# A cross-attention and feed-forward block on one Trainium2 core: the ramp's work in another order, part of w2 loaded from ScalarE's queue, three multiplications on GpSimd

## The chip, the cores and the metric

The kernel runs on one core of one Trainium2 chip. The metric is the device time of one execution in microseconds (us), the median of several runs. Engines: TensorE (PE, matrix products), VectorE (DVE), ScalarE (ACT), GpSimd (POOL) and SyncE (SP), which here only starts transfers. The kernel is written with explicit semaphores: each engine has one list of instructions, worked in the order of the code, and an instruction waits until the semaphores named ahead of it have reached their values.

## The reference

```python
# x (4, 2048, 512), ctx (4, 154, 512); _layernorm is (x - mean) / sqrt(var + eps)
def xattn(x, context, Wq, Wkv, Wout, bout):        # 16 heads of 64
    q = x @ Wq; k, v = split(context @ Wkv)
    mask = j_idx % n_q == i_idx                    # n_q = 2048, n_kv = 154
    sim = where(mask, q k^T * scale, -max)
    return softmax(sim) @ v  @ Wout + bout
def ffn(x, w1, b1, w2, b2, gamma, beta):
    h = layernorm(x, gamma, beta)
    h = qlinear(h, w1, b1)      # y = xq . wq / (sx * sw) + b
    h = gelu(h, approximate=False)
    return qlinear(h, w2, b2)
# act_quant:    scale = 127 / max|x| of the row, xq = round(x * scale)
# weight_quant: scale = 1 / mean|w|, wq = clip(round(w * scale), -1, 1)
x = x + xattn(_layernorm(x), ctx, Wq, Wkv, Wout, bout)
x = x + ffn(_layernorm(x), w1, b1, w2, b2, gamma, beta)
```

Row i below 154 of a batch may see context row i alone, so its attention is that row's value; every other row sees only masked entries, all alike, and gets the mean value of the context. The attention is therefore a row `ctx[i] @ Wv @ Wout + bout` for 154 rows of a batch and one mean row for the others.

## The kernel before

The 8192 rows of x are cut into 64 tiles `t` of 128 rows, rolled by two tiles, so that the first tiles are such that need only batch 0's mean row. The **ramp**, some 100 us, prepares the weights and runs the first tiles between; then a loop over steps `s` runs tile `s`'s first layer and tile `s - 3`'s second layer.

Preparation:
- *Mean row.* TensorE sums batch 0's context (`context_mean`), VectorE scales it (`copy_ctx_mean`). For each of the eight 128-row chunks m of Wv's transpose, `mean_product(m)` (L710) multiplies the chunk with the mean context into one of three buffers `product[m % 3]`, ScalarE's `mean_sum(m)` (L536) sums it along the row, and `mean_weighted(m)` (L717, L721) adds the chunk of Wout times that sum. TensorE's `mean_row` (L990) adds over partitions and VectorE's `mean_row` (L727) writes the result with bout. GpSimd's additions to x wait for it.
- *Wv Wout.* TensorE's `products` (L983) makes `wvo` in 32 products, read from PSUM by ScalarE's `copy_wvo` (L558). `out_rows(i)` (L1008) multiplies a batch's context `ctxm` with wvo, and `attn_rows(i)` (L843) stores it; `tail_product` (L1016) and `tail_rows_out` (L746) serve context rows 128 to 153, with column sums from `ctx_sum` and `ctx_means`.
- *Weights.* w1 comes in eight pieces. ScalarE's `abs_w1(i)` (L543) sums |w| of six, VectorE's (L751) of two. `weight_sum(0)` (L758), TensorE's `weight_total(0)` (L995) and `weight_scale(0)` (L762) give the scale. Then `round_w1` (VectorE, L769) and `round_weights(0, n)` (ScalarE, L553) round, and `clip(0, n)` (VectorE, L779) bounds to -1 and 1. w2 goes the same way in eight pieces: `abs_w2` and `round_weights(1, n)` on ScalarE, `clip(1, n)` on VectorE.

A tile: `add_attention` (GpSimd, L387), `statistics` (VectorE, L784, L786), `inverse_std` (GpSimd, L391, L394), `centre` (VectorE, L792: (x - mean) * gamma), `times_std` (ScalarE, L563), `add_beta` (GpSimd, L402), `x_scale` (VectorE, L797 to L804), `round_x` (ScalarE, L569), `widen_x` and `scale_rows` (GpSimd), a transposing transfer `transpose_x` (SyncE), `bias` and `first_layer` (TensorE, L1030, L1040; 16 products), `gelu` (ScalarE, L578, two halves), `half_scale` and `hidden_scale` (VectorE, L809, L815: row maxima), `round_h` (ScalarE, L587), `transpose_h` (SyncE), `widen_h` in two halves (VectorE L829, ScalarE L596), `second_layer` (TensorE, L1055; 16 products) and `result` (VectorE, L838).

The order in the ramp is written out by hand for each engine: SyncE's from L267, GpSimd's from L439, ScalarE's from L600, VectorE's from L845, TensorE's from L1060. What waits for what around the change:
- `weight_sum(0)` for six abs_w1 on ScalarE and two on VectorE; `weight_total(0)` stands between TensorE's products 30 and 31 of 32.
- `centre(t)` (from t = 6) for `round_x(t - 6)`; ScalarE's `times_std(t)` for `centre(t)` and GpSimd's `inverse_std`.
- `second_layer(0)` for both halves of `widen_h(0)`, for the tail rows, and half by half for the clips of w2; `second_layer(t)` for `widen_h(t)`.
- raw w2 pieces 0 and 3 use the places of x tiles 12 to 15, piece 1 that of the int8 hidden rows, 2 and 4 those of the transposed hidden tiles, 5 to 7 that of Wout, so these wait for `mean_done`, `wvo_done` and the like.

```python
            def out_rows(i):
                b = (i + 1) % B
                pe.wait_ge(wvo_copied, KD)
```

Here `out_rows` needs all four copies of wvo before its first product.

Of the kernel before, what the change touches and what calls it, by code (L numbers as in the profile page):

```python
# [8 lines left out]
ALU = mybir.AluOpType  # L9
# [3 lines left out]
P = 128  # L13
# [5 lines left out]
KD, KI = D // P, INNER // P  # L19
# [14 lines left out]
def block_program(nc, x, ctxm_d, ctxt_d, wvT, wout_d, bout, w1T, b1, w2T, b2, gamma, beta, ctx_b0, out, tail_rows, b1_pieces):  # L34
    es = ExitStack()
    with es:
# [6 lines left out]
        def sem(name):  # L43
            return es.enter_context(nc.semaphore(name))
# [50 lines left out]
        ctx_mean = hx[:, 2, 0, :]  # L95
# [29 lines left out]
        vprod_dve = sem("vprod_dve")  # L125
# [67 lines left out]
        def _(sp):  # L193
# [114 lines left out]
            load_x(9)  # L308
            sp.dma_start(b2_b[:, 0, :], b2.partition_broadcast(P)).then_inc(b2_loaded, 16)
            load_x(10)  # L310
            transpose_x(1)
# [3 lines left out]
            transpose_x(2)  # L315
            transpose_x(3)
            transpose_x(4)
            transpose_h(0)
            transpose_x(5)
            load_x(14)  # L320
            transpose_h(1)
            load_x(15)
# [32 lines left out]
        def _(pool):  # L355
# [94 lines left out]
            inverse_std(2, 2)  # L450
            add_attention(4, 1)
            add_beta(1, 1)
            add_attention(5, 1)
            widen_x(0, 1)
            pool.wait_ge(wscale_done[0], 1)
            scale_rows(0, 1)
            add_beta(2, 1)
            add_beta(3, 1)
            inverse_std(4, 2)
            scale_rows(1, 1)  # L460
            add_attention(6, 1)
            widen_x(1, 1)
            add_beta(4, 1)
            add_beta(5, 1)
            scale_rows(2, 2)
            widen_x(2, 2)
            add_attention(7, 1)
            add_attention(8, 1)
            scale_rows(4, 2)
            add_attention(9, 1)  # L470
            pool.wait_ge(b2_loaded, 16)
            add_b2(0)
            inverse_std(6, 2)
# [49 lines left out]
        def _(act):  # L523
# [92 lines left out]
            copy_wvo(2)  # L616
            times_std(1)
            abs_w1(6)
            abs_w1(7)
            round_x(0)  # L620
            times_std(2)
            times_std(3)
            abs_w2(0)
            copy_wvo(3)
            round_weights(0, 1)
            round_weights(0, 3)
            abs_w2(1)
            times_std(4)
            times_std(5)
            round_x(1)  # L630
            abs_w2(2)
            abs_w2(4)
            abs_w2(3)
# [3 lines left out]
            gelu(0, 0)  # L637
            round_x(2)
            gelu(0, 1)
            round_x(3)  # L640
            round_weights(1, 0)
            round_weights(1, 1)
            round_x(4)
            round_x(5)
            gelu(1, 0)
            gelu(1, 1)
            round_h(0)
            round_weights(1, 2)
            round_weights(1, 3)
            round_weights(1, 4)  # L650
            gelu(2, 0)
            times_std(6)
            gelu(2, 1)
            round_h(1)
            round_weights(1, 5)
            round_weights(1, 6)
            widen_h(0)
            round_weights(1, 7)
            times_std(7)
            gelu(3, 0)  # L660
            gelu(3, 1)
            round_h(2)
# [36 lines left out]
        def _(dve):  # L699
# [148 lines left out]
            mean_product(2)  # L848
# [4 lines left out]
            mean_product(4)  # L853
            mean_product(5)
            mean_weighted(3)
            mean_product(6)
# [10 lines left out]
            statistics(1)  # L867
            statistics(2)
            statistics(3)
            abs_w1(4)  # L870
            centre(1)
            centre(2)
            x_scale(0, 1)
            centre(3)
            statistics(4)
            weight_sum(0)
            centre(4)
            weight_scale(0)
            statistics(5)
            x_scale(1, 1)  # L880
            ctx_sum(0)
            ctx_sum(1)
            ctx_sum(2)
            centre(5)
            x_scale(2, 2)
            attn_rows(0)
            ctx_sum(3)
            round_w1(0)
            round_w1(2)
            clip(0, 0)  # L890
            clip(0, 1)
            clip(0, 2)
            clip(0, 3)
            attn_rows(1)
            attn_rows(2)
            weight_sum(1)
            ctx_means()
            weight_scale(1)
            x_scale(4, 2)
            half_scale(0)  # L900
            statistics(6)
            statistics(7)
            hidden_scale(0)
            half_scale(1)
            statistics(8)
            statistics(9)
            hidden_scale(1)
            centre(6)
            centre(7)
            half_scale(2)  # L910
            attn_rows(3)
            tail_rows_out()
            hidden_scale(2)
            clip(1, 0)
            clip(1, 1)
            clip(1, 2)
            clip(1, 3)
            widen_h(0)
            clip(1, 4)
            clip(1, 5)  # L920
            clip(1, 6)
            clip(1, 7)
# [40 lines left out]
        def _(pe):  # L963
# [117 lines left out]
            tail_product()  # L1081
# [55 lines left out]
```

## Time and profile before

| | |
|---|---|
| median of 3 runs | 539.83 us (539.54 to 540.08) |
| the profiled execution's own time | 540.51 us |
| its span, first to last instruction | 538.7 us |
| mean granted TensorE clock | 0.990 |
| TensorE busy | 527.3 us, 98% |
| VectorE, ScalarE, GpSimd busy | 453.6 (84%), 435.9 (81%), 407.3 (76%) |
| moved by the queues | 78.72 MB, mean 146 GB/s |

Busy time of an engine is the time in which an instruction of it ran. Rows of a timeline give start, length, engine, line of the code, operation, what it writes and reads and how many merged instructions the row holds; "idle before" in square brackets is the engine's idle time ahead of the row and what released it. An fp32 product is two passes on TensorE, so its rows count two. The granted clock is a share of 2.4 GHz. A transfer's time to landing runs from its issue to the last byte.

### The profile page before, as it was taken

Reading aid. Unit: us, or ns where it says so; the run is one execution under the profiler, and the core shown is the slowest. Engines: PE = TensorE matmul, PEld = TensorE weight load, DVE = VectorE, ACT = ScalarE, POOL = GpSimd, SP = SyncE. Lnnn points to the kernel's source line nnn. Section 1 sums busy time; section 2 is a strip of 40 time slices with the busy share of each in tenths; the row PEclk is TensorE's granted clock in tenths of the full one; section 3 lists DMA queues with packets and bytes.
Section 4 is the critical chain, followed back from the end, with each engine's and each line's share of the span. In section 5 each row is a group of like instructions: output and inputs, shape, how many; then the busy total and the mean of one; then the engine's idle time right before and its main releaser. Section 6 shows DMA issues by size and latency. Waiting matters only on the chain.

```text
span 538.7 us, 8129 instructions
## 1 busy us (share of the span) xinstructions
PE 527.3 (98%) x2434; PEld 227.4 (42%) x2434; DVE 453.6 (84%) x758; ACT 435.9 (81%) x444; POOL 407.3 (76%) x533
## 2 busy tenths in 40 slices
PE   9979989999999999999999999999999999999997
PEld 5433434444444444444444444444444444444443
DVE  3877999999989899988888887988888889887653
ACT  3558899888887888888888888888888889887762
POOL 2288687999998888888888988888888888873300
PEclk9987999999999999999999999999999999999999
DMA  8999233886565656555665556665455574535433
GB/s 310 402 387 294 69 69 102 170 208 162 135 122 141 131 148 119 129 125 130 131 143 142 123 129 117 141 132 132 124 123 130 129 142 103 92 86 100 95 78 98
DMA packets 137015, 78.72 MB, mean 146 GB/s; under 512 B 114246, under 2 KB 114310, under 8 KB 136972
## 3 DMA queue, kind: packets, MB, share of 16 engines
q1 hardware_dynamic: 135636, 75.80, 57.3%
q10 hardware_dynamic: 1335, 2.41, 1.3%
q8 instruction: 19, 0.31, 0.2%
q14 instruction: 25, 0.20, 0.1%
HBM read 33.88 MB, written 17.05 MB: 95 GB/s over the span
## 4 chain that ended last, share of the span: by engine, by line
PE 95%; DVE 3%; POOL 1%; ACT 1%; issue 1%; POOLq 0%; DVEq 0%; ACTq 0%
PE py L1055 41%; PE p L1040 28%; PE pab L1040 14%; PE p L983 3%; PE p L1030 3%; PE pab L1008 2%; PE pab L1030 1%; POOL xr L387 1%; PE pab L968 1%; DVE hx L792 1%; PE py L1016 1%; PE py L1008 1%; DVE w2q L779 1%; ACT hid L578 0%; PE py L974 0%
## 5 line engine op out<-in xcount | busy, mean ns | idle before, releaser
L1055 PE MATMUL py<-w2q,hqT 128*128 128x512 bf16 x1024 | 231.0, 379 | 1.7 <-DVE hqT L829 1.7
L587 ACT ACTIVATE hq<-hid,hscale 128x2048 int8<-128x2048 f32 x64 | 128.1, 2002 | 46.2 <-DVE hscale L821 46.2
L1040 PE MATMUL p<-w1q,xqT 128*128 128x512 bf16 x688 | 159.4, 380 | 0.0
L1055 PEld LDWEIGHTS py<-w2q,hqT 128*128 128x128 bf16 x1024 | 100.1, 98 | 123.0 <-DVE hqT L829 2.7
L578 ACT ACTIVATE hid<-p,xdeq 128x1024 f32<-128x1024 f32 x86 | 95.0, 1106 | 15.9 <-PE p L1040 11.2
L1040 PEld LDWEIGHTS p<-w1q,xqT 128*128 128x128 bf16 x688 | 63.8, 98 | 81.2 <-issue 10.1
L387 POOL TENSOR_TENSOR xr<-xr,attn 128x512 f32<-128x512 f32 x64 | 83.3, 1320 | 18.7 <-DVE attn L727 17.2
L402 POOL TENSOR_TENSOR hx<-hx,beta_b 128x512 f32<-128x512 f32 x64 | 91.7, 1454 | 4.4 <-ACT hx L563 4.3
L815 DVE TENSOR_REDUCE hmax<-hid 128x1 f32<-128x1025 f32 x64 | 78.1, 1220 | 18.0 <-ACT hid L578 17.4
L406 POOL TENSOR_TENSOR xr<-xr,b_b 128x512 f32<-128x512 f32 x64 | 92.6, 1465 | 0.0
L809 DVE TENSOR_REDUCE hid<-hid 128x1 f32<-128x1024 f32 x64 | 77.4, 1209 | 8.8 <-ACT hid L578 8.8
L829 DVE CAST hqT<-hT 128x1024 bf16<-128x1024 int8 x64 | 61.5, 962 | 23.4 <-PE py L1055 12.9
L1040 PE MATMUL pab<-w1q,xqT 128*128 128x512 bf16 x336 | 79.6, 380 | 0.0
L596 ACT ACTIVATE hqT<-hT 128x1024 bf16<-128x1024 int8 x64 | 67.0, 1046 | 3.1 <-DMA hT<-hq 3.1
L433 POOL CAST xq<-xq 128x1024 bf16<-128x1024 int16 (+1 forms) x33 | 34.3, 1039 | 44.8 <-ACT xq L569 44.8
L792 DVE SCALAR_TENSOR_TENSOR hx<-xr,mv,gamma_b 128x512 f32<-128x512 f32 x64 | 54.1, 849 | 0.1
L578 ACT ACTIVATE hid<-pab,xdeq 128x1024 f32<-128x1024 f32 x42 | 46.5, 1106 | 7.2 <-PE pab L1040 3.9
L838 DVE SCALAR_TENSOR_TENSOR xr<-py,hdeq,xr 128x512 f32<-128x512 f32 x64 | 47.4, 740 | 3.3 <-PE py L1055 3.3
L1040 PEld LDWEIGHTS pab<-w1q,xqT 128*128 128x128 bf16 x336 | 31.1, 98 | 39.5 <-issue 4.8
L563 ACT ACTIVATE hx<-hx,rstd 128x512 f32<-128x512 f32 x64 | 42.7, 715 | 5.9 <-POOL rstd L394 5.3
L784 DVE BATCH_NORM_STATS2 stat<-xr 128x6 f32<-128x512 f32 x64 | 43.0, 672 | 3.4 <-POOL xr L387 3.3
L569 ACT ACTIVATE xq<-hx,xscale 128x512 int16<-128x512 f32 x64 | 42.6, 714 | 0.1
(88 smaller groups left out, 408.9 us busy)
## 6 DMA issues: line engine op xcount, KB each, us to landing
xr<-x SPq DMA_DIRECT2D x64, 256.0 KB, 2.9
out<-xr SPq DMA_DIRECT2D x64, 256.0 KB, 2.4
raw<-w1T SPq DMA_DIRECT2D x8, 512.0 KB, 12.2
hid<-wvT SPq DMA_DIRECT2D x8, 256.0 KB, 7.8
wout<-wout_d ACTq DMA_DIRECT2D x8, 256.0 KB, 8.7
wout<-w2T SPq DMA_DIRECT2D x3, 512.0 KB, 5.5
xr<-w2T SPq DMA_DIRECT2D x2, 512.0 KB, 11.1
attn<-ctxm_d SPq DMA_DIRECT2D x4, 256.0 KB, 8.1
```

What stands on the lines that cost most here:

```text
L387: pool.tensor_tensor(xtile(t, n), xtile(t, n), a, ALU.add).then_inc(x1_ready, n)
L402: pool.tensor_tensor(htile(t, n), htile(t, n), bb, ALU.add).then_inc(xnormed, n)
L406: pool.tensor_tensor(xtile(t), xtile(t), b2_b[:, :, :], ALU.add).then_inc(xb_ready, 1)
L578: nc.scalar.activation(hid[:, t % 2, h * HALF:(h + 1) * HALF], hidden_pair(t, h), ACT.Gelu, scale=col(xdeq, t)).then_inc(gelu_done, 1)
L587: nc.scalar.activation(hq8[:, t % 2, :], hid[:, t % 2, 0:HID], ACT.Copy, scale=col(hscale, t))\
L596: nc.scalar.activation(hqT[:, t % 2, NJ // 2:, :, :], hT8[:, t % 2, HALF:].rearrange("p (j t e) -> p j e t", e=2, t=P), ACT.Copy).then_inc ...
L792: nc.vector.scalar_tensor_tensor(htile(t)[:, 0, :], xtile(t)[:, 0, :], mv[:, t % 8, 0:1], gamma_b[:, :], ALU.subtract, ALU.mult).then_inc( ...
L809: nc.vector.tensor_reduce(hid[:, t % 2, HID:HID + 1], hid[:, t % 2, 0:HALF], AX.X, ALU.max, apply_absolute_value=True).then_inc(hmax_half, 1)
L815: nc.vector.tensor_reduce(col(hmax, t), hid[:, t % 2, HALF:HID + 1], AX.X, ALU.max, apply_absolute_value=True).then_inc(hmax_done, 1)
L829: nc.vector.tensor_copy(hqT[:, t % 2, 0:NJ // 2, :, :], hT8[:, t % 2, 0:HALF].rearrange("p (j t e) -> p j e t", e=2, t=P))\
L1040: mm = nc.tensor.matmul(hidden_bank(t, n), xT[:, k, :], w1q[:, k, n * D:(n + 1) * D], start=False, stop=(k == KD - 1))
L1055: mm = nc.tensor.matmul(py[:, t % 2, :], hqT[:, t % 2, c // 2, c % 2, :], w2q[:, c, :], start=(c == 0), stop=(c == 2 * NJ - 1))
```

## The change

It does five things.

1. GpSimd makes `mean_product` for chunks 2, 4 and 6, counted by a semaphore of its own; VectorE keeps the other five. ScalarE's `mean_sum` waits for the one or the other.
2. w2's pieces 0 to 4 are started by ScalarE, between its steps; 5 to 7 stay with SyncE.
3. `out_rows` waits for each copy of wvo ahead of the product that reads it.
4. SyncE asks for w1's last pieces before x tile 3, and for the context and b1's rows before x tiles 4 to 6; `transpose_x(1)` to `(3)` and x tiles 14 and 15 move.
5. The lists of all five engines in the ramp are put in another order; on TensorE `out_rows(2)` and `(3)`, `weight_total(1)` and `tail_product` change places with tiles' layers. The loops from step 6 on stay.

```diff
@@ SyncE
-                if j == 3:
-                    sp.wait_ge(mean_done, 1)
...
-            load_x(3)
             load_w1(6)
             load_w1(7)
+            load_x(3)
+            load_ctx()
+            load_b1_rows()
             load_x(4)
-            load_w2(0)
-            load_b1_rows()
             load_x(5)
-            load_w2(1)
-            load_ctx()
-            load_w2(2)
             load_x(6)
-            load_w2(3)
-            load_w2(4)
             transpose_x(0)
             load_w2(5)
             load_w2(6)
+            transpose_x(1)
             load_w2(7)
@@ GpSimd
+            def mean_product(m):
+                pool.wait_ge(chunk_loaded[m], 32)
+                pool.wait_ge(ctx_mean_copied, 1)
+                if m >= 3:
+                    pool.wait_ge(vmean_done, m - 1)
+                pool.tensor_tensor(product[m % 3], wv[:, m // 4, m % 4, :], ctx_mean, ALU.mult).then_inc(vprod_pool, 1)
...
             split_b1()
+            mean_product(2)
+            mean_product(4)
+            mean_product(6)
             pool.wait_ge(mean_copied, 1)
             add_attention(0, 1)
             add_attention(1, 1)
-            add_attention(2, 1)
-            add_attention(3, 1)
             pool.wait_ge(const_set, 3)
             inverse_std(0, 1)
+            add_attention(2, 1)
             inverse_std(1, 1)
@@ ScalarE
+            def load_w2(j):
+                if j == 3:
+                    act.wait_ge(mean_done, 1)
+                act.dma_start(w2raw[j], w2T[j * 2 * P:(j + 1) * 2 * P, :].rearrange("(p e) n -> p e n", e=2))\
+                    .then_inc(w2_loaded[j], 16)
...
-                act.wait_ge(vprod_dve, m + 1)
+                if m in (2, 4, 6):
+                    act.wait_ge(vprod_pool, m // 2)
+                else:
+                    act.wait_ge(vprod_dve, (1, 2, 0, 3, 0, 4, 0, 5)[m])
@@ TensorE
                 b = (i + 1) % B
-                pe.wait_ge(wvo_copied, KD)
...
                 for k in range(KD):
+                    pe.wait_ge(wvo_copied, k + 1)
...
             bias(0)
-            out_rows(2)
             first_layer(0, 0)
             first_layer(0, 1)
-            weight_total(1)
+            out_rows(2)
             bias(1)
             first_layer(1, 0)
+            weight_total(1)
             first_layer(1, 1)
-            out_rows(3)
+            tail_product()
             bias(2)
             first_layer(2, 0)
             first_layer(2, 1)
-            tail_product()
+            out_rows(3)
```

VectorE from the clips of w2 (L779, `w2q<-w2q`) to its fourth `half_scale` (`hid<-hid`), in the order before:

```order
L779 TENSOR_SCALAR w2q<-w2q 128x1024 x4
L829 CAST hqT<-hT 128x1024
L779 TENSOR_SCALAR w2q<-w2q 128x1024 x4
L784 BN_STATS stat<-xr 128x6
L786 BN_AGGR mv<-stat 128x2
L792 SCALAR_TENSOR_TENSOR hx<-xr,mv,gamma_b 128x512
L784 BN_STATS stat<-xr 128x6
L786 BN_AGGR mv<-stat 128x2
L809 TENSOR_REDUCE hid<-hid 128x1
```

and of the change, what stands between the last clip and the same `half_scale`:

```order
L811 SCALAR_TENSOR_TENSOR hx<-xr,mv,gamma_b 128x512
L803 BN_STATS stat<-xr 128x6
L805 BN_AGGR mv<-stat 128x2
L803 BN_STATS stat<-xr 128x6
L805 BN_AGGR mv<-stat 128x2
L811 SCALAR_TENSOR_TENSOR hx<-xr,mv,gamma_b 128x512
L803 BN_STATS stat<-xr 128x6
L805 BN_AGGR mv<-stat 128x2
L811 SCALAR_TENSOR_TENSOR hx<-xr,mv,gamma_b 128x512
L803 BN_STATS stat<-xr 128x6
L805 BN_AGGR mv<-stat 128x2
L828 TENSOR_REDUCE hid<-hid 128x1
```

Before, only statistics(10), centre(8) and statistics(11) stand between the last clip and that row; now it is centre(6) to (8) and statistics(8) to (11). The clips themselves moved ahead, in pairs, among other steps.

ScalarE from its first |w1| sum on (L543 or L557, `w1q,wpart<-raw`), before:

```order
L543 ACTIVATE w1q,wpart<-raw 128x1024
L563 ACTIVATE hx<-hx,rstd 128x512
L543 ACTIVATE w1q,wpart<-raw 128x1024
L558 ACTIVATE wvo<-p 128x512
L563 ACTIVATE hx<-hx,rstd 128x512
L543 ACTIVATE w1q,wpart<-raw 128x1024 x2
L569 ACTIVATE xq<-hx,xscale 128x512
```

and now:

```order
L557 ACTIVATE w1q,wpart<-raw 128x1024
L536 DMA xr<-w2T 128x1024
L536 DMA hq<-w2T 128x1024
L577 ACTIVATE hx<-hx,rstd 128x512
L557 ACTIVATE w1q,wpart<-raw 128x1024
L536 DMA hqT<-w2T 128x1024
L536 DMA xr<-w2T 128x1024
L572 ACTIVATE wvo<-p 128x512
L557 ACTIVATE w1q,wpart<-raw 128x1024
L536 DMA hqT<-w2T 128x1024
L583 ACTIVATE xq<-hx,xscale 128x512 x2
```

Five transfers of w2 stand between the sums of w1's last pieces, and both `round_x` of tiles 0 and 1 follow at once.

## Rows read from the trace of the kernel before

**Rows 1.** Table of stretches: start:end, length, busy (and count) by engine, PEclk, DMA, GB/s.
```profile
22.25:84.51 62.26, 55.21 (x176) 23.03 (x174) 54.05 (x96) 50.85 (x68) 49.60 (x62) 0.92 0.65 215
84.51:103.00 18.49, 18.49 (x92) 7.78 (x88) 18.01 (x30) 16.48 (x17) 16.10 (x20) 1.00 0.57 128
...
120.00:200.00 80.00, 80.00 (x395) 34.27 (x393) 74.60 (x125) 69.01 (x68) 70.39 (x90) 1.00 0.61 139
```

**Rows 2.** Timeline of TensorE, 21 to 107 us.
```profile
21.09 1.05 PE L990 MATMUL py<-xr,hT 128*128 128x512 f32 x2
21.98 12.18 PE L983 MATMUL p<-wout,hid 128*128 128x512 f32 x28
37.66 0.56 PE L995 MATMUL py<-wsum,hT 128*128 128x1 f32 x2 [3.50 <-DVE wsum L758]
38.08 3.76 PE L983 MATMUL p<-wout,hid 128*128 128x512 f32 x4
42.53 9.30 PE L1008 MATMUL pab<-wvo,attn 128*128 128x512 f32 x16 [0.69 <-ACT wvo L558]
...
64.32 3.60 PE L1008 MATMUL py<-wvo,attn 128*128 128x512 f32 x8
...
80.81 3.63 PE L1055 MATMUL py<-w2q,hqT 128*128 128x512 bf16 x16 [1.68 <-DVE hqT L829]
...
103.03 3.63 PE L1055 MATMUL py<-w2q,hqT 128*128 128x512 bf16 x16
```

**Rows 3.** Table of stretches of 2 us, columns as in rows 1.
```profile
36.00:38.00 2.00, 0.34 (x2) 0.37 (x2) 1.97 (x5) 2.00 (x5) 2.00 (x3) 0.67 1.07 401
38.00:40.00 2.00, 2.00 (x5) 0.97 (x5) 1.11 (x4) 1.39 (x3) 2.00 (x3) 0.50 1.03 399
```

**Rows 4.** Timeline of VectorE, 14 to 104 us.
```profile
14.27 1.29 DVE L710 TENSOR_TENSOR hx<-hid,hx 128x512 f32<-128x512 f32 x2
...
22.25 0.69 DVE L727 TENSOR_TENSOR attn<-py,bout_b 128x512 f32<-128x512 f32 x1 [1.29 <-PE py L990]
...
70.00 3.20 DVE L792 SCALAR_TENSOR_TENSOR hx<-xr,mv,gamma_b 128x512 f32<-128x512 f32 x2
...
84.51 1.19 DVE L809 TENSOR_REDUCE hid<-hid 128x1 f32<-128x1024 f32 x1
...
89.40 0.77 DVE L792 SCALAR_TENSOR_TENSOR hx<-xr,mv,gamma_b 128x512 f32<-128x512 f32 x1
...
101.83 1.75 DVE L829 CAST hqT<-hT 128x1024 bf16<-128x1024 int8 x2
```

**Rows 5.** Waits of VectorE, 22 to 103 us: total, times, longest.
```profile
DVE stat L784 <- POOL xr L387: 3.3, 4, 1.8
DVE attn L843 <- PE pab L1008: 2.6, 1, 2.6
```

**Rows 6.** Timeline of GpSimd, 22 to 36 us.
```profile
23.02 4.20 POOL L387 TENSOR_TENSOR xr<-xr,attn 128x512 f32<-128x512 f32 x3 [17.19 <-DVE attn L727]
28.70 1.26 POOL L387 TENSOR_TENSOR xr<-xr,attn 128x512 f32<-128x512 f32 x1 [1.48 <-DMA xr<-x]
```

**Rows 7.** Timeline of ScalarE, 30 to 81 us.
```profile
30.93 0.72 ACT L563 ACTIVATE hx<-hx,rstd 128x512 f32<-128x512 f32 x1 [5.34 <-POOL rstd L394]
...
75.70 2.19 ACT L553 ACTIVATE w2q<-wout,wscale 128x1024 int16<-128x1024 f32 x2
...
79.66 1.13 ACT L553 ACTIVATE w2q<-wout,wscale 128x1024 int16<-128x1024 f32 x1
```

**Rows 8.** SyncE's last issue of w1 and last two of ctxm: ns, first and last start.
```profile
L206 SPq DMA_DIRECT2D raw<-w1T x1: 1123/1123/1123, 19.3 to 19.3; - x1
...
DMA to landing us min/median/max: 11.9/11.9/11.9
...
L220 SPq DMA_DIRECT2D attn<-ctxm_d x2: 432/434/435, 29.9 to 30.4; - x2
...
DMA to landing us min/median/max: 7.4/8.0/8.6
```

More of the change, by code:

```diff
@@ L124, in block_program @@
         ctx_mean_done, ctx_mean_copied = sem("ctx_mean_done"), sem("ctx_mean_copied")
-        vprod_dve = sem("vprod_dve")
+        vprod_dve, vprod_pool = sem("vprod_dve"), sem("vprod_pool")
         vmean_done, mean_part_done = sem("vmean_done"), sem("mean_part_done")
@@ L308, in _ @@
             load_x(9)
+            transpose_x(2)
+            transpose_x(3)
             sp.dma_start(b2_b[:, 0, :], b2.partition_broadcast(P)).then_inc(b2_loaded, 16)
             load_x(10)
-            transpose_x(1)
             load_x(11)
@@ L314, in _ @@
             load_x(13)
-            transpose_x(2)
-            transpose_x(3)
+            transpose_h(0)
+            load_x(14)
+            load_x(15)
+            transpose_h(1)
             transpose_x(4)
-            transpose_h(0)
             transpose_x(5)
-            load_x(14)
-            transpose_h(1)
-            load_x(15)
             transpose_h(2)
@@ L449, in _ @@
             add_beta(0, 1)
-            inverse_std(2, 2)
-            add_attention(4, 1)
             add_beta(1, 1)
-            add_attention(5, 1)
+            add_attention(3, 1)
             widen_x(0, 1)
@@ L456, in _ @@
             scale_rows(0, 1)
+            inverse_std(2, 2)
+            widen_x(1, 1)
+            scale_rows(1, 1)
             add_beta(2, 1)
             add_beta(3, 1)
+            add_attention(4, 1)
+            scale_rows(2, 2)
+            add_attention(5, 1)
+            add_attention(6, 1)
+            widen_x(2, 2)
             inverse_std(4, 2)
-            scale_rows(1, 1)
-            add_attention(6, 1)
-            widen_x(1, 1)
+            add_attention(7, 1)
             add_beta(4, 1)
             add_beta(5, 1)
-            scale_rows(2, 2)
-            widen_x(2, 2)
-            add_attention(7, 1)
             add_attention(8, 1)
@@ L470, in _ @@
             add_attention(9, 1)
+            inverse_std(6, 2)
             pool.wait_ge(b2_loaded, 16)
             add_b2(0)
-            inverse_std(6, 2)
             add_attention(10, 1)
@@ L615, in _ @@
             abs_w1(5)
-            copy_wvo(2)
+            load_w2(0)
+            load_w2(1)
             times_std(1)
             abs_w1(6)
+            load_w2(2)
+            load_w2(3)
+            copy_wvo(2)
             abs_w1(7)
+            load_w2(4)
             round_x(0)
+            round_x(1)
+            round_weights(0, 1)
+            copy_wvo(3)
+            round_weights(0, 3)
             times_std(2)
@@ L623, in _ @@
             abs_w2(0)
-            copy_wvo(3)
-            round_weights(0, 1)
-            round_weights(0, 3)
             abs_w2(1)
-            times_std(4)
-            times_std(5)
-            round_x(1)
             abs_w2(2)
+            abs_w2(3)
+            gelu(0, 0)
             abs_w2(4)
-            abs_w2(3)
+            gelu(0, 1)
+            round_x(2)
+            round_x(3)
             abs_w2(5)
@@ L636, in _ @@
             abs_w2(7)
[L637 to L644, printed above, removed]
             gelu(1, 0)
             gelu(1, 1)
+            round_weights(1, 0)
+            times_std(4)
+            times_std(5)
+            round_weights(1, 1)
             round_h(0)
@@ L649, in _ @@
             round_weights(1, 3)
+            gelu(2, 0)
             round_weights(1, 4)
-            gelu(2, 0)
-            times_std(6)
             gelu(2, 1)
@@ L655, in _ @@
             round_weights(1, 5)
+            round_x(4)
+            round_x(5)
+            widen_h(0)
             round_weights(1, 6)
-            widen_h(0)
             round_weights(1, 7)
-            times_std(7)
             gelu(3, 0)
             gelu(3, 1)
+            times_std(6)
+            times_std(7)
             round_h(2)
@@ L847, in _ @@
             mean_product(1)
-            mean_product(2)
             mean_product(3)
@@ L852, in _ @@
             mean_weighted(2)
-            mean_product(4)
             mean_product(5)
             mean_weighted(3)
-            mean_product(6)
             mean_product(7)
@@ L867, in _ @@
             statistics(1)
+            centre(1)
+            abs_w1(4)
             statistics(2)
-            statistics(3)
-            abs_w1(4)
-            centre(1)
             centre(2)
             x_scale(0, 1)
-            centre(3)
[L875 to L880, printed above, removed]
+            weight_sum(0)
+            x_scale(1, 1)
+            weight_scale(0)
+            round_w1(0)
+            clip(0, 0)
+            statistics(3)
+            centre(3)
+            clip(0, 1)
+            round_w1(2)
+            clip(0, 2)
+            clip(0, 3)
+            attn_rows(0)
             ctx_sum(0)
@@ L883, in _ @@
             ctx_sum(2)
-            centre(5)
[L885 to L900, printed above, removed]
+            x_scale(2, 2)
+            ctx_sum(3)
+            attn_rows(1)
+            half_scale(0)
+            ctx_means()
+            hidden_scale(0)
+            statistics(4)
+            weight_sum(1)
+            centre(4)
+            weight_scale(1)
+            attn_rows(2)
+            statistics(5)
+            centre(5)
+            half_scale(1)
+            hidden_scale(1)
+            clip(1, 0)
+            clip(1, 1)
             statistics(6)
             statistics(7)
-            hidden_scale(0)
-            half_scale(1)
+            x_scale(4, 2)
+            tail_rows_out()
+            clip(1, 2)
+            clip(1, 3)
+            half_scale(2)
+            hidden_scale(2)
+            clip(1, 4)
+            clip(1, 5)
+            widen_h(0)
+            attn_rows(3)
+            clip(1, 6)
+            clip(1, 7)
+            centre(6)
             statistics(8)
             statistics(9)
-            hidden_scale(1)
-            centre(6)
             centre(7)
[L910 to L922, printed above, removed]
             statistics(10)
```

## The prediction

> **What bounds the kernel now.** I read the table of stretches first, then TensorE's rows of the ramp with the granted clock, then what VectorE and ScalarE waited for. TensorE is busy 80.00 of 80.00 us in the steady part, and 18.49 of 18.49 already from 84.51 on [rows 1]. The change touches nothing that TensorE does there. So only the ramp can give time, and only if `second_layer(3)`, which starts at 103.03 [rows 2], starts earlier and no gap opens behind it.
>
> TensorE's losses in the ramp stand as idle time in its rows: 3.50 us ahead of `weight_total(0)` at 37.66, 0.69 ahead of `out_rows(0)`, 1.68 ahead of `second_layer(0)` at 80.81 [rows 2]. The long one has a second price. The granted clock is 0.67 in 36 to 38 and 0.50 in 38 to 40 [rows 3]: it fell to 1.2 GHz inside that gap. The four passes behind it took 3.76 where 28 took 12.18 (1.74 for four), and sixteen passes of `out_rows` took 9.30 where eight at 2.4 GHz take 3.60 [rows 2]: 2.0 and 2.1 more. With these three gaps TensorE alone could win 10 us.
>
> It is not alone. `second_layer(3)` needs VectorE's `widen_h(3)`, the first of two casts that fill 101.83 to 103.58 [rows 4]; TensorE comes to it at 103.0 straight from tile 6. Both arrive together, and VectorE is busy 18.01 of the 18.49 us before [rows 1]. The end is held twice, and the second holder is VectorE's list.
>
> **The decisive step: VectorE's list.** From `mean_row` (22.25) to `half_scale(3)` (84.51) [rows 4] both orders hold the same work (statistics 0 to 11, centre 0 to 8, all clips, attn_rows 0 to 3), arranged differently; from `half_scale(3)` to `widen_h(3)` nothing is moved. The three multiplications that leave VectorE lie ahead of 22.25, where it waits 1.29 for TensorE anyway [rows 4]: they give nothing here. In the stretch VectorE is busy 54.05 of 62.26 [rows 1] and idle 8.2: 3.3 and 2.6 are its two large waits [rows 5], 2.3 small waits and the short steps between dependent instructions. The change can give 8.2 minus the idle time that it leaves.
>
> **New times, step by step.**
> GpSimd makes `inverse_std(0)` behind two additions, not four. Three additions take 4.20 from 23.02; the fourth ends at 29.96 [rows 6], and ScalarE's `times_std(0)` follows at 30.93 [rows 7], 0.97 later. Now it is 23.02 + 2.80 + 0.97 = 26.8; ScalarE's 5.34 us of waiting go. Late next is the rest of ScalarE's own list up to the last abs_w1: three of these at the 1.05 of a 1024-column step (two take 2.19 with 0.1 of overlap [rows 7]), two small steps and copy_wvo, some 0.6 each, and four DMA issues. An issue is 0.43 on SyncE [rows 8]. That is 26.8 + 3.15 + 1.8 + 1.7 = 33.5. w1's last piece landed at 31.2 (19.3 + 11.9 [rows 8]) and is now asked for before x tile 3. `weight_sum(0)` so moves from 37.4 to 33.6, TensorE is free at 34.16, and the 3.50 us gap closes, with it the fall of the clock.
>
> The products end at 36.2. The context has to be in; it was at 39.0 (30.4 + 8.6 [rows 8]). It now stands right behind x tile 3, 1.2 MB after 31.2, which is 3.1 us at the 400 GB/s that rows 3 show: 34.3 alone. But w2's pieces 0 and 1 (1 MB, 2.6 us) enter beside it on ScalarE's queue: 36.9. The DMA share is 1.07 and the rate 401 GB/s in 36 to 38 [rows 3]: the pipe is full, so a second queue only lets w2 in ahead of what SyncE's queue holds. I take 0.8 us of TensorE waiting at `out_rows(0)`, ends 0 and 2.6; the five issues cost ScalarE 5 x 0.43 = 2.2. The Trainium skill, "DMA: Bandwidth & Descriptors", section "Issuing engines are not separate DMA queues", goes against this part in the same way: starting transfers from several engines saves issue time only. By that rule it gains nothing on the wire and moves issue time from an idle queue to a busy engine; the trace's full rate agrees.
>
> From 37.0: two `out_rows` 7.2, tile 0's layer 3.9, `out_rows(2)` 3.6, half of tile 1's layer 2.1: 53.8. `weight_total(1)` needs all eight abs_w2, and ScalarE's list (two large roundings, four small steps, eight abs, two gelu) ends there too. Then half a layer, and `gelu(1,1)` is done at 56.9. Behind it ScalarE has, without a wait, eight roundings and two gelu at 1.05, four small steps at 0.6, two `round_h` of twice that width at 1.9 and a `widen_h` of 1: 17.7. The last of w2 is rounded at 74.6; it was 80.7 (79.66 + 1.13, less overlap [rows 7]). `second_layer(0)` starts near 73.
>
> But 6 us won there are not 6 us. In the old order centre(6) and (7) and statistics(6) to (9) were done **ahead** of the w2 clips, in time in which VectorE would have waited for ScalarE. Now centre(6), statistics(8), (9), centre(7), statistics(10), centre(8), statistics(11) follow clip(1,7). Four statistics at about 0.8, and three centres at 0.77 (alone) to 1.60 (3.20 for two, beside GpSimd [rows 4]), are 5.5 to 8.0, which puts `half_scale(3)` at 80.5 to 83.0. The other account goes by waits: 0.3 before statistics(0), 1.0 around weight_sum(0), 0.9 before weight_sum(1), 3.8 where clips 5 to 7 come at ScalarE's pace, and 1.5 for what lies between dependent instructions: 7.5. Then 22.25 + 54.05 + 7.5 = 83.8. I take 83.8, since 54.05 contains the real stretching of this ramp by other engines, and the chain's single durations don't. That is 0.7 us before 84.51.
>
> **The three products on GpSimd.** No such multiplication is in the trace. The nearest row is GpSimd's addition of the same shape, 1.26 alone and 1.40 as one of three [rows 6]. VectorE's last step of that chain ends at 20.96 (22.25 less 1.29), and TensorE would take its result from 21.09 on [rows 2]: 0.1 us of cover. The gain can't be used. The cost is bounded by what a centre shows for two-input work on both engines, 0.8 more each (1.60 against 0.77), 2.4 for three, less the 1.9 that VectorE no longer does (three at 0.65, as in the 1.29 for two [rows 4]). I take 0.3; ends 0 and 0.9, a gain being excluded because TensorE's products last to 21.1. The Trainium skill, "GPSIMD Engine Reference", section "Key points", says that GpSimd shares its SBUF interfaces with VectorE and contends with instructions that have two SBUF inputs. The rows of the centres agree. By that rule alone this part would cost VectorE about what it saves.
>
> **Sum.** -0.7 for VectorE's list, +0.3 for the mean row: -0.4. The profiled execution took 540.51 (span 538.7) and would take 540.1. The median of the runs, 539.83, lies 0.68 below it and goes to 539.4. A measurement of this kernel can tell about 0.2%, 1.1 us, from no change, so the likeliest case would hardly be seen.
>
> **Rivals.**
> *The clock falls later (slower).* TensorE does `second_layer(0)` in two halves, the second behind clip(1,7), to 77, then tile 4 in 3.85: 81. `second_layer(1)` needs `widen_h(1)`, behind `half_scale(3)`: 83.8 + 1.1 + 0.6 = 85.5. A gap of 4 to 5 us opens where there was none. The gap of 3.50 brought the clock down [rows 2, 3]; behind the one of 1.68 sixteen passes took 3.63, as at 2.4 GHz [rows 2]. If it falls again for as long (products and two `out_rows` were hit, till some 46 us), some 8 us of work run at 1.2 GHz and lose 4.1. The slack: 85.5 and two tile steps of 7.4 (three take 22.22 from 80.81 to 103.03 [rows 2]) are 100.3, against 102.2 for VectorE. It decides once 1.9 are lost, that is 3.8 us of slow work. 100.3 + 4.1 = 104.4, 1.4 later than 103.03, and 0.3 for the mean row: 541.5; ends 540.3 and 542.5. For it: the length of the gap. Against: a ScalarE that lags moves TensorE into the gap and shortens it.
> *The centres run free (faster).* With `half_scale(3)` at 80.5, 4.0 us are to be had; ScalarE, busy 16.48 of 18.49 [rows 1], has 2.0 of room. So 2.0 to 2.5 go: 537.5. For it: the chain's own low end. Against: GpSimd has additions queued through the whole stretch.
> *Nothing moves (no change).* The context is 2.6 late, the products cost 0.9, the waits only change places: 539.8.
>
> **Chances.** Forecast 0.42, clock 0.25, free centres 0.20, nothing moves 0.13. Of the forecast 0.08 lie past 1.1 us faster; of the clock case 0.22 past 1.1 slower. Faster 0.28, same 0.50, slower 0.22. The range leaves out the outer ends of the two outer cases: 537.3 to 541.9; the forecast's own is 538.4 to 540.2.
>
> **What would show it.** Right: no idle before `weight_total(0)`, a clock of 1.00 in 36 to 48, `second_layer(0)` before 76, `half_scale(3)` at 83 to 84.5, a TensorE gap of 3 to 5 us before `second_layer(1)` put down to the hqT cast, `second_layer(3)` near 102.3. A clock of 0.5 somewhere in 83 to 93 shows the first rival. The forecast is wrong if `half_scale(3)` comes before 82.5, if TensorE shows gaps behind 110, or if the mean row is copied later than 22.8.

## The result: 0.94% slower, outside the range

| | before | after |
|---|---|---|
| median of the runs | 539.96 us (4 runs, 539.54 to 541.34) | 545.38 us (4 runs, 541.82 to 547.08) |
| ratio, 95% interval | | 1.0094 [1.0061, 1.0127] |
| second set of runs | 539.63 us (23 runs) | 545.73 us (6 runs), 1.0091 [1.0059, 1.0124] |

The forecast was 539.4, with a range up to 541.9. The profiled execution of the changed kernel was the fastest of its four, 541.82 us, and shows little of the loss. A second profile of the same kernel took 545.64 us and is typical. Both are read here: they run the same program, and what differs between them points to the cause. TensorE in the typical execution (start, length, engine, line, what it writes and reads, passes, idle before; a row of x7 lacks the record of one pass):

```profile
7.75 14.00 PE L999 MATMUL p<-wout,hid 128*128 128x512 f32 x32
...
34.53 0.28 PE L1011 MATMUL py<-wsum,hT 128*128 128x1 f32 x2
34.67 1.96 PE L999 MATMUL p<-wout,hid 128*128 128x512 f32 x4
41.49 8.66 PE L1024 MATMUL pab<-wvo,attn 128*128 128x512 f32 x16 [4.86 <-DMA attn<-ctxm_d]
...
60.24 0.35 PE L1011 MATMUL py<-wsum,hT 128*128 128x1 f32 x2 [0.60 <-DVE wsum L777]
...
79.85 1.90 PE L1071 MATMUL py<-w2q,hqT 128*128 128x512 bf16 x7 [2.87 <-DVE hqT L848]
...
91.21 3.63 PE L1071 MATMUL py<-w2q,hqT 128*128 128x512 bf16 x16 [0.72 <-DVE hqT L848]
...
107.88 3.63 PE L1071 MATMUL py<-w2q,hqT 128*128 128x512 bf16 x16 [1.82 <-DVE hqT L848]
```

The same in the execution that took 541.82:

```profile
8.12 15.70 PE L999 MATMUL p<-wout,hid 128*128 128x512 f32 x32 [1.33 <-DMA wout<-wout_d]
...
36.53 0.28 PE L1011 MATMUL py<-wsum,hT 128*128 128x1 f32 x2
36.67 1.96 PE L999 MATMUL p<-wout,hid 128*128 128x512 f32 x4
38.47 7.03 PE L1024 MATMUL pab<-wvo,attn 128*128 128x512 f32 x16
...
56.25 0.35 PE L1011 MATMUL py<-wsum,hT 128*128 128x1 f32 x2 [1.27 <-DVE wsum L777]
...
76.20 5.31 PE L1071 MATMUL py<-w2q,hqT 128*128 128x512 bf16 x16 [3.20 <-DVE hqT L848]
...
87.58 3.63 PE L1071 MATMUL py<-w2q,hqT 128*128 128x512 bf16 x16 [2.18 <-DVE hqT L848]
...
104.25 3.63 PE L1071 MATMUL py<-w2q,hqT 128*128 128x512 bf16 x16 [1.82 <-DVE hqT L848]
```

In both, the gap of 3.50 us ahead of `weight_total(0)` and the slow passes behind it [rows 2] are gone, as the change meant: `weight_total(0)` runs at 34.53 instead of 37.66. In the typical execution 4.86 us of waiting for the context (`ctxm_d`) stand in their place, and sixteen passes take 8.66, not 7.03, behind it, since the granted clock falls in the wait (table of stretches of the typical execution, columns as in rows 1):

```profile
34.00:40.00 6.00, 2.63 (x8) 0.98 (x6) 5.76 (x12) 5.58 (x5) 4.65 (x8) 1.00 1.03 392
40.00:44.00 4.00, 2.51 (x3) 1.18 (x4) 2.26 (x3) 3.25 (x6) 3.78 (x8) 0.65 1.16 281
```

The other execution has no such wait. Its first product waited 1.33 for a load and its 32 passes took 15.70 instead of 14.00, so its mean row came 2.06 later, and yet it was the faster one. My reading, from this one pair of executions: **the late start helped**. ScalarE issues w2's loads behind steps that wait for the mean row, so a late mean row holds w2 back and the context goes ahead. ScalarE's issues in the typical execution, then in the other:

```profile
27.39 0.33 ACTq L536 DMA_DIRECT2D xr<-w2T  x1
27.76 0.46 ACTq L536 DMA_DIRECT2D hq<-w2T  x1
29.87 0.34 ACTq L536 DMA_DIRECT2D hqT<-w2T  x1
```

```profile
29.38 0.35 ACTq L536 DMA_DIRECT2D xr<-w2T  x1
29.76 0.45 ACTq L536 DMA_DIRECT2D hq<-w2T  x1
31.87 0.33 ACTq L536 DMA_DIRECT2D hqT<-w2T  x1
```

SyncE issues the context's pieces at nearly the same times in both; what differs is the time to landing. Typical, then the other:

```profile
L218 SPq DMA_DIRECT2D attn<-ctxm_d x4: 599/1615/2569, 21.3 to 26.5; - x4
...
DMA to landing us min/median/max: 11.7/12.7/14.9
```

```profile
L218 SPq DMA_DIRECT2D attn<-ctxm_d x4: 663/1444/2553, 21.4 to 26.7; - x4
...
DMA to landing us min/median/max: 9.0/9.8/10.9
```

The last piece, issued at 26.5 and 26.7, took 14.9 and 10.6: it landed at 41.4, where TensorE's wait ends, and at 37.3, before TensorE came for it at 38.47. Who moved the bytes in the typical execution while the context was under way, 27.4 to 41.4 us (q1 is SyncE's queue, q10 ScalarE's; packets, MB, share of the 16 DMA engines):

```profile
q1 hardware_dynamic: 1822, 2.82, 56.1%
q10 hardware_dynamic: 719, 2.62, 48.2%
```

The two shares make 1.04: the wire was full, at (2.82 + 2.62) / 14.0 = 0.389 MB per us, and w2, needed by ScalarE from 41.99 at the earliest, took nearly half of it. At that rate the 2.62 MB are worth 6.7 us of SyncE's queue.

What a delay here costs is shown by the profiles together. In twelve of the fourteen profiles of this study the span is the start of `second_layer(3)` plus 435.6 to 435.9 (before: 538.7 - 103.03 = 435.7; typical: 543.7 - 107.88 = 435.8); the other two are 436.0 and, told below, 437.3. Of the 5.13 us between the typical execution and before's profiled one (545.64 - 540.51), 4.85 are the later start of `second_layer(3)` (107.88 - 103.03).

### The profile page after: what moved, and what is told of

The parts are those of the page before. It is cut to its first block, busy times and chain, and to the rows that moved or that the text cites. A ratio compares the mean times of both kernels' runs of the same rounds, so it can differ in the third digit from the quotient of the medians.

```text
span 539.9 us, 8129 instructions
## 1 busy us (share of the span) xinstructions
PE 525.8 (97%) x2434; PEld 226.9 (42%) x2434; DVE 455.4 (84%) x755; ACT 436.5 (81%) x444; POOL 413.9 (77%) x536
## 4 chain that ended last, share of the span: by engine, by line
PE 84%; DVE 9%; ACT 2%; issue 2%; POOL 2%; DMA 1%; ACTq 0%; DVEq 0%; POOLq 0%
PE py L1071 39%; PE p L1056 25%; PE pab L1056 13%; PE p L999 3%; PE p L1046 2%; DVE hx L811 2%; PE pab L1046 1%; DMA wout<-wout_d 1%; ACT w2q L567 1%; DVE stat L803 1%; DVE hmax L834 1%; DVE xmax L816 1%; DVE hqT L848 1%; DVE hid L828 1%; ACT hq L601 1%
## 5 line engine op out<-in xcount | busy, mean ns | idle before, releaser
L592 ACT ACTIVATE hid<-p,xdeq 128x1024 f32<-128x1024 f32 x86 | 95.1, 1106 | 15.7 <-PE p L1056 10.9
L403 POOL TENSOR_TENSOR hx<-hx,beta_b 128x512 f32<-128x512 f32 x64 | 90.1, 1431 | 2.1 <-ACT hx L577 2.0
L1056 PE MATMUL pab<-w1q,xqT 128*128 128x512 bf16 x336 | 79.6, 380 | 0.0
```

Source lines behind the costliest of these rows:

```text
L403: pool.tensor_tensor(htile(t, n), htile(t, n), bb, ALU.add).then_inc(xnormed, n)
L592: nc.scalar.activation(hid[:, t % 2, h * HALF:(h + 1) * HALF], hidden_pair(t, h), ACT.Gelu, scale=col(xdeq, t)).then_inc(gelu_done, 1)
L1056: mm = nc.tensor.matmul(hidden_bank(t, n), xT[:, k, :], w1q[:, k, n * D:(n + 1) * D], start=False, stop=(k == KD - 1))
```

## The experiments

Ratios are to the kernel before on the same chip, with their 95% interval.

**The same kernel again, and the products back on VectorE.** First the changed kernel as it is, on another chip.

> The changed kernel once more, nothing edited. Its four runs took 541.82, 545.35, 545.41 and 547.08, the profiled one being the fastest. If the slowdown is one of the first loads (TensorE's first product waited 1.3 us and the clock was 0.5 from 8.3 to 11.7 in that profile), the runs should spread again between 539.5 and 547 and the mean row's copy should start between 22.3 and 25. If the slowdown lies in the order (gaps ahead of second_layer(0), (1) and (3)), a slow run shows the mean row in time and longer gaps from 70 us on. Median 542 to 546 by either.

545.73 us, 1.0091 [1.0059, 1.0124]: the loss is the kernel's. Its profile is the typical one above. Then with the three multiplications on VectorE, and all else as changed:

```diff
-            mean_product(2)   # GpSimd
-            mean_product(4)
-            mean_product(6)
+            mean_product(2)   # VectorE, likewise 4 and 6
-                if m in (2, 4, 6):
-                    act.wait_ge(vprod_pool, m // 2)
...
+                act.wait_ge(vprod_dve, m + 1)
```

> The changed kernel with all eight products of Wv with the mean context on VectorE, as before. If GpSimd's products are what delays the mean row (24.78 against 22.25), the row comes at 22.3 and the time falls by some 2.5 us, to 539.5 to 541. If they only move idle time, the time stays with the full change, 542 to 546.

545.71 us, 1.0096 [1.006, 1.0133]. The products are not the cause.

**Each part alone in the kernel before.** Only the products on GpSimd; then only the new order, w2 staying on SyncE's queue; then only w2's five loads on ScalarE's queue.

> The kernel before with GpSimd's three products alone. If the products delay the mean row: slower by 1 to 2.5 us (541 to 542.5). If they are covered by TensorE's products, as forecast: 539.8 to 540.3, mean row copied at 22.2 to 22.6.

539.83 us, 0.9987 [0.9967, 1.0007].

> The changed order alone: products back on VectorE, w2's first pieces back on SyncE's queue. If the order is the cause of the slowdown: 542 to 546. If it is one of the two other parts: 538.5 to 540.5.

541.0 us, 1.0017 [0.9995, 1.0039].

> The kernel before, with w2's first five pieces issued by ScalarE from 31 us on (behind its sixth, seventh and eighth abs_w1). If w2 is taken out of SyncE's line, the context there is 1 MB further ahead, but shares the wire. If the late start of these loads matters less than in the changed order: 539 to 540.5. If the second queue costs by itself: 542 to 545.

539.43 us, 0.9985 [0.9966, 1.0005]. None of the parts costs 0.9% alone. Now in pairs, first the new order with the products on GpSimd and w2 back on SyncE's queue:

```diff
+            load_w2(0)        # SyncE, behind load_x(4); 1 to 4 behind load_x(5) and (6)
-            load_w2(0)        # ScalarE; 1 to 4 likewise
```

> The changed kernel with w2's first five loads back on SyncE's queue: the new order and GpSimd's products, without a second queue. If the loss is the second queue pushing the context's last piece back (5 us late in the profiled execution of the changed kernel on its second chip), nothing waits for the context here, second_layer(3) starts near 104 as with the order alone, and the time is 541 (540.3 to 541.7), ratio 1.000 to 1.004. If order and GpSimd's products together hurt (GpSimd's additions start later and everything behind them in VectorE's list), it stays above 543 with no wait for the context.

540.66 us, 1.0019 [1.0, 1.0037].

Then the old order with both other parts:

> The kernel before with both other parts, GpSimd's products and the five w2 loads on ScalarE's queue, in the old order. Each alone measured 0.9987 and 0.9985 with intervals that hold 1. If both are nothing in this order: 539 to 540, ratio 0.998 to 1.001. If they are small gains that add up: 538.3, ratio 0.997. If the loads on the second queue are harmful whatever the order, as a theory of a busy wire alone would have it, the context's last piece lands behind 38 and the time is over 541.

539.88 us, 1.0007 [0.9986, 1.0029].

| | w2 on SyncE's queue | w2 on ScalarE's queue |
|---|---|---|
| old order | 1 | 0.9985 |
| old order, products on GpSimd | 0.9987 | 1.0007 |
| new order | 1.0017 | 1.0096 |
| new order, products on GpSimd | 1.0019 | 1.0091 (the change; first set 1.0094) |

The table narrows the cause down: **the second queue costs 0.7 to 0.8% in the new order, and nothing that these runs can tell in the old.** Two things differ between the orders there, and the table can't divide them. The first is the room that the context has. In the old order `out_rows(0)` waits for ScalarE's last `copy_wvo` [rows 2] and no profile shows it waiting for the context; the new order brought TensorE there 4 to 6 us earlier, and made the context urgent. The second is when w2 is issued. In the old order ScalarE comes to w2's loads at 31.9 and 32.6 us, 2.9 and 2.5 behind the issue of the context's last piece, which then took 7.8 and 8.5 to land, no longer than before's 8.6 [rows 8]. In the typical execution of the change it comes to them at 27.39, 0.9 behind that issue, and the piece took 14.9. So in these two profiles of the old order, both of late starts, the second queue did not delay the context at all.

In the profile of the new order with w2 on SyncE's queue the context is in time: its last piece takes 8.3 and lands at 35.6, 1.5 before TensorE comes.

```profile
35.16 0.28 PE L1013 MATMUL py<-wsum,hT 128*128 128x1 f32 x2
37.10 7.03 PE L1026 MATMUL pab<-wvo,attn 128*128 128x512 f32 x16
45.79 0.39 PE L1048 MATMUL p<-b1rows,xqT 32*128 32x512 bf16 x4 [1.66 <-DMA xqT<-xq]
...
55.95 0.35 PE L1013 MATMUL py<-wsum,hT 128*128 128x1 f32 x2 [0.61 <-DVE wsum L779]
...
103.59 3.63 PE L1073 MATMUL py<-w2q,hqT 128*128 128x512 bf16 x16 [1.82 <-DVE hqT L850]
```

`weight_total(1)` runs at 55.95 against 60.24, `second_layer(3)` at 103.59 against 107.88: 4.29 both times. What is lost until 60 us is not made up: in all ten profiles of the new order `second_layer(3)` starts 47.6 to 48.3 behind `weight_total(1)`.

**Where the w2 loads are put.** All five behind `copy_wvo(3)` on ScalarE, past the context's landing:

```diff
             copy_wvo(3)
+            load_w2(0)        # 1 to 4 likewise; their early places are empty
```

> The changed kernel, with all five w2 loads of ScalarE issued together behind copy_wvo(3), near 38 to 40 us, instead of from 27 us on. If the context's transfers were late because w2 takes its share of the transfer engines in 27 to 40 us: no wait ahead of out_rows(0), clock 1.00 there, and a time like that of the order alone, 540 to 541.5. If it is ScalarE's issue time or the second queue as such that costs: 544 to 546 as in the full change. New risk: abs_w2(0) would wait about 1 us for its data.

546.18 us, 1.0101 [1.0072, 1.0129]: a miss. The profiled execution, 544.31, was the fastest of its six, so it shows a part of the loss only. The context was in time (landed at 35.3), and the loss came by another wait:

```profile
36.70 7.03 PE L1024 MATMUL pab<-wvo,attn 128*128 128x512 f32 x16
47.39 0.61 PE L1046 MATMUL p<-b1rows,xqT 32*128 32x512 bf16 x4 [3.66 <-DMA xqT<-xq]
...
106.69 3.63 PE L1071 MATMUL py<-w2q,hqT 128*128 128x512 bf16 x16 [1.81 <-DVE hqT L848]
```

This time ScalarE's queue was in the way of `transpose_x(0)`, issued at 38.25. The queues in 38.0 to 47.4 us, and the transposes' time to landing:

```profile
q10 hardware_dynamic: 711, 2.58, 77.8%
q1 hardware_dynamic: 736, 0.43, 22.4%
```

```profile
DMA to landing us min/median/max: 2.6/4.2/9.1
```

38.25 + 9.1 is 47.35, where TensorE's wait ends. With w2 on SyncE's queue that transpose took 7.1. TensorE comes out of the wait 1.60 later than there (47.39 against 45.79) and loses another 1.5 in tile 0's layer, which runs at a granted clock of 0.54 and 0.60 in 47 to 51 us; `second_layer(3)` is 3.10 later. My theory had been too narrow: w2 delays not only the context, but the transpose too, if that is what SyncE's queue holds. With two pieces early and three late:

> The dose: only w2's pieces 0 and 1 stay early on ScalarE's queue, pieces 2 to 4 go behind copy_wvo(3). By the shared rate, 1 MB ahead of the context instead of up to 2.5 MB: the last context piece lands near 38 and out_rows(0) waits 1 to 2 us in place of 4.9 (the forecast's own assumption was this case); time 541 to 543. If the count of bytes doesn't matter: 545 to 546.

542.35 us, 1.0039 [1.0022, 1.0056], between the 1.0019 with no piece on ScalarE's queue and the 1.0091 with all five early. The interval overlaps that of the former, and the three late pieces can cost something of their own, so the time alone doesn't show that the loss grows with the bytes. The context's last piece shows it better. From issue to landing it took 8.3 or 8.4 in the four profiles of the new order without the second queue, 14.5 and 14.9 with five pieces early, and with two (least, median and most of the context's four pieces; the most is the last piece's):

```profile
DMA to landing us min/median/max: 7.7/8.7/10.9
```

That is 2.5 to 2.6 and 6.1 to 6.6 more, and two and five pieces are 1.05 and 2.62 MB, 2.6 and 6.6 us at 0.4 MB per us. It is no law: five pieces cost 2.3 in the execution of 541.82, where they began 2.7 behind the context's last issue. The profile with two pieces started late too (15.70 for the products). The context landed at 38.7 in it and `out_rows(0)` began at 38.80 with no idle time ahead of it; it doesn't show what an execution on time would wait. `bias(0)` waited 1.80 in it for the transpose. Last, the changed kernel with the context moved ahead of x tile 3:

```diff
-            load_x(3)
             load_ctx()
+            load_x(3)
```

> The changed kernel with the context's loads ahead of x tile 3's on SyncE's queue. If the context is late because SyncE's queue has to move a fixed number of bytes at the share of the wire that ScalarE's five loads leave it (in 28 to 34 us it moved 1.50 MB of 2.32), then 0.26 MB less ahead of it bring its last piece in 1.0 us earlier: the wait at out_rows(0) falls from 4.9 to 3.9 or a little less, and the time to 544.7. If its lateness is set by something else (the descriptors of its own pieces, when they were issued), the wait stays 4.2 to 4.9 and the time 545.7.

545.15 us, 1.01 [1.0068, 1.0133]. The time is 0.6 less than the kernel's own on another chip, but the ratios show no gain (1.01 against 1.0091), and the profile tells another story than my sum. The execution started late (15.70 for the products), so its context would have been in time without the edit too. In the nearest execution to compare, the one of 541.82, GpSimd adds to x tile 3 at 34.26 without a wait. Here:

```profile
32.29 2.50 POOL L403 TENSOR_TENSOR hx<-hx,beta_b 128x512 f32<-128x512 f32 x2
39.07 1.80 POOL L388 TENSOR_TENSOR xr<-xr,attn 128x512 f32<-128x512 f32 x1 [4.27 <-DMA xr<-x]
```

Behind that addition stand GpSimd's row scales of tile 0, so `transpose_x(0)` is issued at 43.42 instead of 40.03, and `inverse_std(2)`, for which ScalarE waits 3.42 (0.84 there):

```profile
45.83 1.33 ACT L577 ACTIVATE hx<-hx,rstd 128x512 f32<-128x512 f32 x2 [3.42 <-POOL rstd L395]
```

`second_layer(3)` starts at 107.24. Context, x tile 3 and the first transpose are each needed at once in the new order: with w2 on ScalarE's queue the profiles show waits of 4.86 and 4.15 for the first, 4.27 for the second and 3.66 for the third.

**What the new order gives by itself.** Centre(6) and (7) ahead of the clips, w2 on SyncE's queue, products on VectorE:

```diff
             tail_rows_out()
+            centre(6)
+            centre(7)
             clip(1, 2)
...
             clip(1, 7)
-            centre(6)
             statistics(8)
             statistics(9)
-            centre(7)
```

> The order alone, with centre(6) and (7) moved back ahead of the w2 clips, as they stood before. If VectorE's list as a whole sets second_layer(3) (same work, only its waits count): ScalarE's waits for them (3.5 us) and the gap ahead of second_layer(1) go, and the time stays within 1 us of the order alone (541.0). If the gap ahead of second_layer(1) is itself the cost: faster by 1 to 2 us, 539 to 540.

541.12 us, 1.0019 [0.9997, 1.004], as with the order alone. TensorE's gap before `second_layer(1)` went, and no time with it. This is the profile whose span is `second_layer(3)` plus 437.3. It started at 102.61, 1.55 earlier than with the order alone (0.88 of that is an earlier mean row), behind a gap of 2.10 us, and ran slowly:

```profile
102.61 5.29 PE L1070 MATMUL py<-w2q,hqT 128*128 128x512 bf16 x16 [2.10 <-DVE hqT L844]
```

```profile
102.00:104.00 2.00, 1.39 (x4) 0.56 (x5) 2.00 (x4) 2.00 (x2) 2.00 (x3) 0.65 0.48 163
104.00:106.00 2.00, 2.00 (x7) 0.60 (x6) 1.93 (x5) 2.00 (x3) 2.00 (x3) 0.50 0.67 182
```

Granted clock 0.65 and 0.50, that is 1.2 GHz; the passes took 1.66 more. Behind a gap of 1.80 with the order alone they took 3.63 at 1.00. To see whether this ate the gain, in the same kernel eight passes over constant data in the gap:

```diff
             def second_layer(t, first=0, last=2 * NJ):
+                if t == 3:
+                    pe.wait_ge(y_ready, t - 1)
+                    for c in range(8):
+                        nc.tensor.matmul(py[:, t % 2, :], w2q[:, c, 0:P], w2q[:, c, :], start=True, stop=True)
```

> The earlier run with centre(6) and (7) ahead of the clips, and ahead of second_layer(3) eight matmuls over constant data that fill TensorE's idle time there (their result is overwritten by second_layer(3)'s first pass). That run started second_layer(3) at 102.61, 1.55 earlier than the order alone, but its sixteen passes took 5.29 instead of 3.63 behind a gap of 2.10 us, with a granted clock of 0.65 and 0.50. If that fall of the clock ate the gain: no fall here, sixteen passes in 3.63, and 539.5 (541.12 less 1.66). If the fall was an accident of that one profiled execution (its median of 541.12 would then need another cause): 541.1 again.

540.25 us, 1.0015 [0.9995, 1.0035]. The passes did take 3.63, and the clock stayed at 1.00, but `second_layer(3)` started at 103.08, and the ratio can't be told from 1.0019. Whether the clock's fall cost the medians anything stays open. No version beat the kernel before.

## Why the prediction was wrong

**The step that failed is the wait at `out_rows(0)`**: "I take 0.8 us of TensorE waiting at `out_rows(0)`, ends 0 and 2.6". It measured 4.86 and 4.15 in the two profiles of this order and queue whose mean row was on time (21.59 and 21.89 on TensorE). I had the mechanism, a full wire on which a second queue only lets w2 in ahead, but put w2's pieces 0 and 1 beside the context and not 2 to 4. They are issued from 29.87 to 30.82, and the context lands at 41.4, so all five, 2.62 MB, shared the wire with it; the bound had to be 2.62 MB / 0.4 = 6.6 us. A transfer that shares a wire is itself later, and so meets more of the other queue; the sum ended the overlap at the time that it took without the overlap. The two parts that it did hold came out: without the second queue the context landed at 34.7 and 35.6 (34.3 forecast), and two pieces alone made its last piece 2.6 later, as put. In an execution on time that would be 26.5 + 10.9 = 37.4 against TensorE at 36.6, the forecast's 0.8; this is an estimate, no profile shows it.

**The second failure is where the delay went.** I added the wait to TensorE's account and took VectorE's list, from 22.25 on, as the holder of the end, so that TensorE's waits would be absorbed. VectorE's largest waits in the typical execution, 22 to 104 us, show otherwise (total, times, longest):

```profile
DVE attn L862 <- PE pab L1024: 4.5, 1, 4.5
DVE wsum L777 <- ACT w2q L562: 1.8, 1, 1.8
DVE hid L828 <- ACT hid L592: 1.5, 1, 1.5
```

It waits 4.5 for `out_rows(0)` itself (2.6 before [rows 5]) and then for ScalarE, which waited 6.16 for tile 0's layer. The list can't run ahead of TensorE here. Nor did VectorE's list hang on the mean row in the old order: with the row copied at 22.25, 24.70, 24.77 and 25.38, `half_scale(3)` starts at 84.51, 83.70, 84.03 and 84.55.

Point by point:
- The gap of 3.50 us and its clock fall go: **right**. `weight_total(0)` at 34.53 against 34.2 forecast, granted clock 1.00 until the context is missed.
- VectorE's list is 0.7 shorter: the **size came out, the meaning did not**. Mean row to the cast for `second_layer(3)` is 22.25 to 101.83 before, 79.6 [rows 4]; 79.0 and 78.6 in the new order with w2 on SyncE's queue. But in the three old-order profiles with a late mean row it is 76.3 to 76.6, so the stretch is no property of the list, and no time was gained by it.
- `half_scale(3)` at 83 to 84.5: 89.37 in the typical execution, 85.74 in the other, 85.07 without the second queue. The mean row's copy, to be no later than 22.8, stood at 22.78 and 24.78.
- `second_layer(0)` near 73 and `weight_total(1)` at 53.8: too early by 6.9 and 6.4 us in the typical execution, and by 2.6 and 2.2 without the second queue (75.55, 55.95). A part of the latter is the x transpose, for which TensorE waits 1.66 ahead of `bias(0)` and which my chain left out.
- Five issues cost ScalarE 2.2: they took 1.94 on its queue, but beside its steps. Its sum of |w1| starts at 28.01, before the second issue ends (27.76 + 0.46).
- The products cost 0.3: **0**. From the first product to the mean row are 13.84 us (7.75 to 21.59) against 13.83 (7.26 to 21.09) before. My bound, 2.4 less 1.9, was 0.5; the upper end of 0.9 had no working behind it.
- The gap before `second_layer(1)`: seen, 2.18 and 0.72 instead of 3 to 5. The clock fell elsewhere: behind the wait for the context (0.65 in 40 to 44 us), and in the 541.82 execution at `second_layer(0)`, 5.31. The rival "the clock falls later" had the sign; its place and its price were others, and it is not the cause of the loss.
- A gain of 0.4 for all: the order without the second queue gives +0.17 and +0.19%, both intervals reaching to 1. One reading is that the old order absorbs a late mean row and the new one doesn't: old-order profiles with TensorE's mean row at 23.57 to 24.25 start `second_layer(3)` at 102.22 to 103.07, as the one with 21.09 does at 103.03; in the new order it starts at 103.59 for 22.18 and 104.16 for 23.25. The rows suggest how: in the late old-order profiles the gap ahead of `weight_total(0)` is 1.98 to 2.09, not 3.50, and `out_rows(0)` and `(1)` take 7.13, not 9.30. So part of what the change took away, a late start had taken away already. This was not tried by itself.

## What to carry to other kernels

When a change removes a wait on one engine, list what that engine needs next and when each transfer of it lands: a load that had slack becomes urgent, and others on a second queue, if they start early enough, take its wire. Bound what a second queue can cost by all its bytes up to the delayed landing, divided by the full rate, and not by those issued before the landing without it; it is a bound, and loads that start later cost less. Judge such a pair of edits as a pair, since neither alone could be told from nothing here.

## What the runs showed of the hardware

- Two queues on a full wire shared its bytes nearly evenly in one stretch (2.82 and 2.62 MB in 14.0 us) and not in another: with a transpose at the head of SyncE's queue, ScalarE's took 2.58 of 3.0 MB in 9.4 us, in 711 packets against 736. The Trainium skill, "DMA: Bandwidth & Descriptors", section "Issuing engines are not separate DMA queues", says that all of them interleave on the same 16 engines and only issue time is saved; the traces agree (w2 and the context moved at the same time, 0.389 MB per us in all), and add that SyncE's transfers were later for it, by up to 6.6 us.
- TensorE's first product waited 0.4 to 1.6 us for its load in twelve of the fourteen profiles, whatever the kernel. In seven of these the granted clock fell (0.57 in 8 to 12 us of the execution of 541.82) and its 32 passes took 15.6 to 15.7 instead of 14.00; behind waits of 1.25 and 1.35 it did not. In the changed kernel such a start came with the fastest execution.
- The granted clock fell to 1.2 GHz at a gap of 2.10, one of 2.87 and one of 3.20 us (sixteen passes in 5.29, 4.99 and 5.31), and did not in gaps of 1.80 to 1.83. Behind one of 2.48 and another of 2.87, in other executions, the passes ran at full speed (3.63 for sixteen, 1.90 for half). The length of a gap alone did not tell.
